# Four streams on one core: masked copy on ScalarE, division on GpSimd, a shorter root, ternary weights on VectorE, and a written-out order of work

## The reference, cut to what matters

```
x = x + tanh(g_xattn[l]) * attention_l(ctx, layernorm(x))
x = x + tanh(g_ffn[l])   * ffn_l(layernorm(x))
```

```
h = gelu(bitlinear(x, w1, b1)); y = bitlinear(h, w2, b2)
bitlinear: xn = x * rsqrt(mean(x*x) + 1e-6)
           xq = round(xn * 127 / max|xn|) ...;  wq = clip(round(w / mean|w|), -1, 1) * mean|w|
```

## Time and profile before

| | |
|---|---|
| time, median of 3 runs | 2720.06 us (2715.66 to 2722.37) |
| profiled execution, its own time | 2716.3 us |
| its span, first to last instruction | 2714.5 us |
| PE busy | 2508.9 us, 92% |
| DVE busy | 1688.8 us, 62% |
| ACT busy | 1041.0 us, 38% |
| POOL busy | 976.1 us, 36% |
| granted TensorE clock, mean | 0.975 |

### The profile page before, as it was taken

One profiled execution on the slowest core, in us unless ns is written; L12 is line 12 of the kernel. 1 busy time (PEld: TensorE's weight loads), 2 busy tenths in 40 slices (PEclk: granted clock), 3 DMA queues, 4 the chain that ended last, 5 costly groups with the idle time before them and its releaser, 6 DMA issues.

```text
span 2714.5 us, 53760 instructions
## 1 busy us (share of the span) xinstructions
PE 2508.9 (92%) x21317; PEld 1693.2 (62%) x21317; DVE 1688.8 (62%) x4598; ACT 1041.0 (38%) x1654; POOL 976.1 (36%) x2413
## 2 busy tenths in 40 slices
PE   6999788999999988899999998889999998889999
PEld 4566444677767644577776754457776765446776
DVE  6545888755533588955543478885554358887542
ACT  4544345432234445523224444542322444453221
POOL 2352522444332332243442243233444323224342
PEclk8999889999999999999999999999999999899999
DMA  3200100000000000000000000000000000000000
GB/s 125 81 11 1 52 32 14 1 9 9 9 9 12 12 2 14 1 1 9 9 9 9 11 12 1 12 1 9 9 9 9 11 1 12 1 1 1 5 5 8
DMA packets 16280, 37.38 MB, mean 14 GB/s; under 512 B 1408, under 2 KB 11424, under 8 KB 15008
## 3 DMA queue, kind: packets, MB, share of 16 engines
q1 hardware_dynamic: 16032, 33.94, 3.5%
HBM read 29.74 MB, written 4.19 MB: 13 GB/s over the span
## 4 chain that ended last, share of the span: by engine, by line
PE 69%; DVE 22%; ACT 4%; issue 3%; POOL 2%; DMA 0%; SPq 0%; DVEq 0%; ACTq 0%; POOLq 0%
PE P L1322 8%; PE P L1134 4%; PE P L1142 4%; PE P L1181 4%; PE P L1355 4%; PE P L1323 4%; PE P L1193 4%; PE P L1340 4%; PE P L1114 4%; PE P L1331 4%; PE P L1035 4%; DVE mx L1721 4%; PE P L1206 3%; PE P L1031 2%; PE P L1044 1%
## 5 line engine op out<-in xcount | busy, mean ns | idle before, releaser
L1721 DVE TENSOR_REDUCE mx<-P 128x8 f32<-128x1232 f32 x256 | 369.0, 1441 | 178.1 <-PE P L1040 85.9
L1322 PE MATMUL P<-xT,w 128*128 128x256 f32 x1024 | 264.8, 381 | 0.7 <-DVE R L1956 0.3
L1477 ACT ACTIVATE ET<-P 128x2048 f32<-128x2048 f32 x96 | 180.2, 1877 | 162.4 <-PE P L1117 115.3
L1772 DVE SCALAR_TENSOR_TENSOR x<-P,w_first,x 128x512 f32<-128x512 f32 x96 | 73.9, 769 | 252.8 <-PE P L1181 87.0
L1322 PEld LDWEIGHTS P<-xT,w 128*128 128x128 f32 x1024 | 192.0, 190 | 60.7 <-issue 34.9
L792 POOL TENSOR_TENSOR sm<-sm 128x2 f32<-128x2 f32 x384 | 76.0, 198 | 421.0 <-DVE sm L1717 401.0
L1949 DVE SCALAR_TENSOR_TENSOR gu<-gu,P 128x256 f32<-128x256 f32 x128 | 53.9, 421 | 256.7 <-ACT gu L1528 256.7
L1035 PE MATMUL P<-KB,R 32*128 32x308 f32 x1536 | 162.0, 492 | 34.5 <-ACT ET L1477 14.7
L1528 ACT ACTIVATE gu<-P 128x256 f32<-128x256 f32 x128 | 49.2, 384 | 355.9 <-PE P L1323 334.4
L1114 PE MATMUL P<-R,KB 32*128 32x256 f32 x2048 | 169.6, 417 | 14.9 <-DVE mx L1721 14.8
L1434 ACT ACTIVATE xn<-x,sm 128x256 f32<-128x256 f32 x256 | 139.1, 592 | 100.9 <-POOL sm L800 100.9
(11 more groups left out here) (307 smaller groups left out, 5580.8 us busy)
## 6 DMA issues: line engine op xcount, KB each, us to landing
kvw<-in_wkv SPq DMA_DIRECT2D x12, 672.0 KB, 3.9
x<-in_x SPq DMA_DIRECT2D x16, 256.0 KB, 2.8
out<-x SPq DMA_DIRECT2D x16, 256.0 KB, 2.1
w<-in_w SPq DMA_DIRECT2D x2, 1024.0 KB, 5.9
w<-in_wexp SPq DMA_DIRECT2D x1, 1028.0 KB, 7.6
w_w<-in_wcon SPq DMA_DIRECT2D x1, 1024.0 KB, 9.9
w_w<-in_m3t SPq DMA_DIRECT2D x1, 1024.0 KB, 8.3
w<-in_w1q SPq DMA_DIRECT2D x1, 1024.0 KB, 10.3
```

What stands on the lines that cost most here:

```text
L1322: e.matmul(o, wm[:, c, js], s.xT[:, c, :], start=n == c == 0, stop=False, skip_group_check=True)
L1477: e.activation(ET[:].rearrange("p g c -> p (g c)"), quad.rearrange("p g c -> p (g c)"), ACT.Exp, bias=mb1[:, b:b + 1] if l == 1 else 0.0). ...
L1721: e.tensor_reduce(s.mx[:, i, :, 2 * u:2 * u + 2], quad[:, :, 0:2 * NK].rearrange("p g (a k) -> p g a k", a=2), AX.X, ALU.max).then_inc(q_d, 1)
```

## The change

1. `no` in layers 1 to 3 is split. DVE's part ends with the first transpose. A new part of ACT copies the two halves of the bank, each under its mask column, into a new tile VS in the stream's scratch, which frees the bank; one VS serves both halves u, so the second copy waits for POOL's product of the first. A new stage `nz` has the reciprocals and the transpose back on DVE, and a product of 128x512 and the sum of the halves on POOL.
2. The root in `gelu2` works on -x/2 as `norm` does, and each of its steps is done for the two rows of a partition in instructions of one element, so that an instruction waits for the last but one and not for the one ahead of it.
3. `tern` is whole on DVE; SP and PE wait for `d_quant` in place of `g_tern`.
4. The order of each queue no longer comes from `BACK`. A string for each engine (`TURN`) names, item by item, the stream whose next item goes into that engine's queue. The strings came from a local search with new costs in `parts`. A stream may have 64 items open, not 24, stage `val` no longer follows `key` in the plan, and `fill` may also go into the first part of the kernel.

```diff
+            s.VS = part(512, [512])
...
+        TURN = {
+            "PE":
+                "0323232002323232322322010222200110330331030030310130202210012111112120323212102302123222323221032231"
...
-                while i in live and len(queue[i]) < 24:
+                while i in live and len(queue[i]) < 64:
...
-                i, p = min(can, key=lambda c: (start(c[1]) + BACK[c[1][2]].get(c[1][1], 0) + 130.0 * count[c[0]] + 34.0 * c[0],
-                                               count[c[0]] + 0.3 * c[0]))
+                i, p = min((c for c in can if TURN[c[1][2]][taken[c[1][2]]] == str(c[0])), key=lambda c: start(c[1]))
+                taken[p[2]] += 1
...
-                if p[2] == "PE" and at - free["PE"] > 900.0 and done.get("folded") and let["bank"]:
+                if p[2] == "PE" and at - free["PE"] > 900.0 and let["bank"]:
...
-            def tern(c):
-
-                raw, to = ((w1r, w1i), (w2r, w2i))[c]
-                e.wait_ge(d_quant, c + 1)
-                e.tensor_scalar(raw, raw, wsc[:, 4 + c:5 + c], MAGIC, ALU.mult, ALU.add).then_inc(g_tern, 1)
-                e.wait_ge(g_tern, 3 * c + 1)
-                e.tensor_scalar(raw, raw, -MAGIC, 1.0, ALU.add, ALU.min).then_inc(g_tern, 1)
-                e.wait_ge(g_tern, 3 * c + 2)
-                e.tensor_scalar(to[:].rearrange("p a b -> p (a b)"), raw, -1.0, None, ALU.max).then_inc(g_tern, 1)
...
+            def nz(s, b, l, u):
+                t = s.Z[u]
+                e.wait_ge(s.d_o, C.up(s.d_o))
+                e.wait_ge(s.a_q, 13 * b + 3 * l + 3 + u)
+                e.tensor_tensor(t, t, s.VS, ALU.mult).then_inc(s.g_z, 1)
+                e.wait_ge(s.g_z, C.up(s.g_z))
+                e.tensor_tensor(s.OT[:, u, :], t[:, 0:256], t[:, 256:512], ALU.add).then_inc(s.g_p, 1)
                 C.up(s.g_p)
...
-                    free[k] = [(s.d_o, X.up(s.d_o))]
+                    X.up(s.d_o)
+                    X.up(s.d_a)
+                    free[k] = [(s.a_q, X.up(s.a_q))]
...
+            def no(s, b, l, u, k):
+
+                e.wait_ge(s.d_a, C.up(s.d_a))
+                if u:
+
+                    e.wait_ge(s.g_z, 10 * b + 3 * l)
+                for a in range(2):
+                    t = e.activation(s.VS[:, 256 * a:256 * a + 256], P[:, k, 256 * a:256 * a + 256], ACT.Copy,
+                                     scale=tm[:, 2 + a:3 + a])
+                t.then_inc(s.a_q, 1)
...
+                e.tensor_scalar(raw, raw, wsc[:, 4 + c:5 + c], MAGIC, ALU.mult, ALU.add).then_inc(d_own, 1)
+                e.wait_ge(d_own, C.up(d_own))
+                e.tensor_scalar(raw, raw, -MAGIC, 1.0, ALU.add, ALU.min).then_inc(d_own, 1)
+                e.wait_ge(d_own, C.up(d_own))
+                e.tensor_scalar(to[:].rearrange("p a b -> p (a b)"), raw, -1.0, None, ALU.max).then_inc(d_quant, 1)
...
+                if l:
+                    e.transpose(t, bank).then_inc(s.d_a, 1)
+                    C.up(s.d_a)
+                    return
...
-                    for a in range(2):
-                        h = t[:, 256 * a:256 * a + 256]
-                        t_ = e.scalar_tensor_tensor(out=h, in0=bank[:, 256 * a:256 * a + 256], scalar=tm[:, 2 + a:3 + a],
-                                                    in1=h, op0=ALU.mult, op1=ALU.mult)
-                    t_.then_inc(s.d_o, 1)
...
+            def nz(s, b, l, u):
+                t = s.Z[u]
+                T, z = t.rearrange("p (a b c) -> p a b c", a=2, c=32), s.z[:].rearrange("p (a b) -> p a b", a=2)
+                e.wait_ge(s.d_a, C.at(s.d_a))
+                C.up(s.g_z)
+
+                for a in range(2):
+                    e.reciprocal(z[:, a, :], T[:, a, :, 16 - 16 * a]).then_inc(d_own, 1)
+                e.wait_ge(d_own, C.up(d_own, 2))
+                e.transpose(t, s.z[:].unsqueeze(2).broadcast_to([128, 16, 32])).then_inc(s.d_o, 1)
...
+                def own(t, of):
+
+                    t.then_inc(d_own, 1)
+                    e.wait_ge(d_own, C.up(d_own) - of)
+
...
+                own(e.tensor_scalar(hv, ss, 1.0 / 1024.0, 1e-6, ALU.mult, ALU.add), 0)
+                own(e.tensor_scalar(a.bitcast(i32), hv.bitcast(i32), 1, None, ALU.logical_shift_right), 0)
+                own(e.tensor_scalar(hv, hv, -0.5, None, ALU.mult), 1)
+                own(e.tensor_scalar(y.bitcast(i32), a.bitcast(i32), -1.0, 1597463007.0, ALU.mult, ALU.add), 0)
+                for n in range(3):
+                    for i in range(2):
+                        own(e.tensor_scalar(a[:, i:i + 1], y[:, i:i + 1], y[:, i:i + 1], hv[:, i:i + 1], ALU.mult, ALU.mult), 1)
+                    for i in range(2):
+                        own(e.tensor_scalar(y[:, i:i + 1], a[:, i:i + 1], 1.5, y[:, i:i + 1], ALU.add, ALU.mult), 1)
+
+                for i in range(2):
+                    own(e.tensor_scalar(am2[:, i:i + 1], am2[:, i:i + 1], y[:, i:i + 1], 1e-5, ALU.mult, ALU.max), 1 - i)
+                own(e.reciprocal(f, am2), 0)
+                own(e.tensor_scalar(sq, am2, wsc[:, 7:8], None, ALU.mult), 1)
+                for i in range(2):
+                    own(e.tensor_scalar(f[:, i:i + 1], f[:, i:i + 1], 127.0, y[:, i:i + 1], ALU.mult, ALU.mult), 1 - i)
```

More of the change, by code:

```diff
@@ L326, in late @@
                 return [("near", of[0], of[1] - 2)]
+            if engine == "POOL" and name == "no" and of[2] == 0:
+                return [("values", of[3])]
+            if name == "no" and engine == "ACT" and of[3]:
+                return [("divided",)]
+            if name == "nz" and engine == "POOL":
+                return [("copied", of[3])]
             if name == "hw" and of[1] == 6:
@@ L354, in early @@
                 return name, *of
+            if engine == "ACT" and name == "pv":
+                return "values", of[3]
+            if engine == "ACT" and name == "no":
+                return "copied", of[3]
+            if engine == "POOL" and name == "nz" and of[3] == 0:
+                return ("divided",)
             if engine == "DVE" and name in ("h1", "h2"):
@@ L531, in turns @@
                 yield "store", s, b
-        BACK = {"PE": {"back": 258, "down": 825, "exa": 222, "f3": 142, "gate1": -1154, "gate3": 710, "grow": -1683,
-                "h1": 298, "h2": -1734, "key": -1624, "lin": 1269, "mt": -537, "mw": -879, "near": 945, "out":
-                -1537, "pv": 383, "pz": 419, "q1": 260, "q2": -420, "qp": -3861, "sc": 286, "st": 693, "sts": 548,
-                "tsum": -183, "turn": -148, "up": 827, "upt": 383, "val": -555, "w1": -2247, "w2": -497},
-                "ACT": {"ex": 20, "gate1": -307, "gate3": 416, "gelu2": 1098, "h1": 335, "h2": 899, "key": -414,
-                "mt": 268, "mw": -3456, "near": 1412, "norm": 1319, "pv": -616, "q1": 2008, "q2": 944, "qp": 695,
-                "sts": 33, "tl": 802, "turn": 715, "up": -563, "val": 1578, "wide": 1273},
-                "DVE": {"down": 2589, "e3": -1428, "exa": 312, "f3": -1372, "gate1": 1049, "gate3": 95, "gb": -1063,
-                "gelu2": 3285, "grow": -1183, "h1": -3449, "h2": 365, "lin": 1331, "masks": -170, "mx": 917, "near":
-                1117, "no": 1568, "norm": 181, "out": 588, "q1": 1272, "q2": 1256, "split": 990, "tern": -1664,
-                "top1": 2363, "tsum": -740, "upt": -438, "val": 1642, "w1": 708, "w2": 1204, "wide": 1172},
-                "POOL": {"bias": 3534, "hw": -2455, "key": 2928, "mw": 1867, "no": 1720, "norm": 348},
-                "SP": {"kvw": -673, "late": -842, "store": -1615}}
@@ L851, in hw @@
                 C.up(s.g_p)
-            stages = {"key": key, "norm": norm, "bias": bias, "no": no, "mw": mw, "hw": hw, "tern": tern}
+            stages = {"key": key, "norm": norm, "bias": bias, "no": no, "nz": nz, "mw": mw, "hw": hw}
             for name, *of in ORDER["POOL"]:
```

169 lines of the change are left out of this document (98 added, 71 removed).

## The result

The changed kernel takes 2702.7 us (median of 5 runs, 2698.2 to 2707.8) against 2719.3 before (5 runs, 2715.6 to 2722.4): a ratio of 0.9943, 95% interval 0.9925 to 0.9961. It is faster by 16.6 us, a quarter of the 65 forecast, and lies 0.7 us above the forecast's range. Of the cases that were written down it is nearest to the rival in which POOL's products take back what the split gives (2690).

What follows compares the result with a forecast made beforehand. It took DVE to set the pace in the dips and PE elsewhere. 33 (DVE relief) + 7 (`tern`) + 25 (order) = 65 us off 2716.3 gave 2651, forecast as a 2655 us median, range 2600 to 2702.

Steps and rivals of the forecast that it cites:

- the rival in which POOL's products take back what the split gives: POOL's products hold DVE at SBUF, 60 x 0.8 us, cancelling the 48 us: 2690 us, chance 0.19.
- The relief: `no` split: two products of 0.80 us a pair leave DVE, 60 pairs in the dips, 48 us.
- the dips: Four stretches, 870 us together, streams in attention 2 and 3 and feed-forward 1 and 2; DVE 88% busy, PE has gaps.
- the factor of 0.7: Share of DVE's relief in the dips counted for the end: 47 us become 33, bounds 0.3 and 1.
- One product of POOL can thus cost DVE between 0 and 1.27 us. I take 0.2.: POOL's new product in `no` stalls small DVE SBUF instructions: 60 x 0.2 = 12 us, bounds 0 and 76.
- The path from bank to OT grows from 3.5 us to about 3.9.: Split `no`: POOL's product takes 1.27 us where DVE's took 0.80; a few us of PE waiting, not priced separately.
- The third rival: Hand-offs exposed at the end of 48 attentions in layers 1 to 3, 2 us each: 2751 us, slower, chance 0.09.
- The root: `gelu2` on DVE: overlapping small steps take 3.0 us, 0.7 less, x 16 = 11 us, all in the dips.
- `tern`: Ternary weights on DVE, 4.4 us for three passes, POOL no longer holding DVE: 7 us, bounds 2 and 15.
- The lists: Written-out queue order and early `fill`: a tenth of 245 us of PE gaps and `fill`, 25 us.
- In the dips DVE sets the pace: DVE is nearly full there while 199 us are free of useful PE work; outside them PE sets the pace.
- The bounds: Limits on the end's gain from DVE work removed in the dips: 5 to 69 us around 33.

Runs made afterwards that it cites:

- experiment 8: Changed kernel with POOL's product cut to 2 columns, plus POOL zeros or scratch products: behind the halves' sum 2673.9 or 2683.5 us, ahead of it 2685.0 or 2690.8.

## Why the prediction was wrong

The step that failed is the split of `no` with its order, above all in the two prices that it put on the detour over ACT and POOL: a path of 3.9 us, which is 7.3, and 8 us at the end for POOL's product, whose removal moves the end by 26. The forecast booked 48 us off DVE less 12 for POOL's hold, times 0.7, 25 us gained, and 25 more for the order. Measured, the split with its order loses 18 us against the same kernel without both (2702.7 and 2680.9, ratios 0.9943 and 0.9877). The runs don't divide this loss between the two. Point by point:

- *The relief.* "60 pairs x 0.80 = 48 us": with the products cut to 2 columns the end moves by 17 us for 30 of DVE in the dips, but PE's wait behind the same path shrank by 10, so the factor of 0.7 is neither confirmed nor refuted.
- *"One product of POOL can thus cost DVE between 0 and 1.27 us. I take 0.2."* DVE's busy time falls by 20.3 us when the product goes, 0.21 for each of 96: the price was right. What it does to the end was not. The forecast took it as 60 x 0.2 x 0.7 = 8 us. Narrowing the product moves the end by 26, of which products that nobody waits for reproduce 9, and products in its place 15. Some 15 of the profiled 27.5 us are PE's own matmuls at a higher granted clock, a term that the sum did not have.
- *"The path from bank to OT grows from 3.5 us to about 3.9."* It grew to 7.3. The sum added durations of instructions and no queues: DVE, ACT, DVE and POOL in turn, each with other streams' work in front. A microsecond more of zeros on each pair's path costs 11 us at the end (experiment 8). "I leave it in the factor below" was the mistake.
- *The third rival* has this mechanism and said that it decides from 1.35 us for each attention. In the old order the kernel is 95 us slower, with PE 61 us in front of `out`; in the new order that wait is 2.7 us.
- *The root.* Forecast 11 us off the stage and 8 at the end. Measured, 14 off the stage alone and 21 in the changed kernel, and 27 and 19 at the end. The overlap of the steps was the smaller part: without a stall the stage went from 3.80 to 3.48 us, not by the 0.7 forecast. The larger part was not in the sum: the 3.70 us of the old root left out one stalled instruction as an exception, and stalls were the rule (5.05 us on average, 12 of 16 turns stalled). The new root is stalled for less of its time. At the end, 10 of the 24.6 us between the profiled executions are shorter gaps and 14 are PE's own matmuls at a higher granted clock; what raised the clock is not shown. One factor of 0.7 for everything on DVE did not hold.
- *`tern`.* Forecast 7, measured 10 (7 to 14). Right, with its reasons.
- *The lists.* Forecast 25 us and a few from the clock. The early filling gives 6. The rest of the order can't be priced apart from the stages; what it shows is that it hides the split's path (61.3 us of PE's wait down to 2.7), and beyond that no gain appeared in the dips.
- *"In the dips DVE sets the pace"* did not hold as it stands. DVE's narrow products and its root gained time, but each also shortened a path that PE waits for, so they don't tell load from path. In the changed kernel DVE's time fell by 38 us with PE's gaps unchanged, while the stage's own path grew.
- *The bounds.* "With the bounds above 5 to 69": the 5 does not follow. With POOL's price at its own bound of 76 the split alone stands at 48 - 76 = -28 us, so the sum allowed for a loss that its range left out.

So the sum would have read: root 27, `tern` 10, filling 6, less 10 of overlap, less 18 for the split with its order, 15 us in all. The 65 forecast had 50 us on the split and the order.

## What to carry to other kernels

Work that is moved off a busy engine is a chain with one more hand-off for each engine it visits. Price the queue in front of each, from the mean of all instances of the stage and not from the sum of its instructions. Read a stage's time as the mean over all its instances, stalls included, for the instance that looks undisturbed is the one that misleads. And take each part of a change apart before keeping it: here three small parts are worth 33 us, and the large one takes 18 back. Where the granted clock can move, compare PE's own matmul time beside its gaps before a cause is named.

## What the runs showed of the hardware

VectorE `tensor_scalar` instructions on one element, with scalars from columns, were not held by POOL: all 96 of L1907 took 262 to 275 ns, and of the new root's one-element instructions in that kernel 69 overlapped in time with a POOL instruction of two SBUF operands. On two elements a `tensor_tensor` of the old root lasted up to 1194 ns where its median is 161, and a `tensor_scalar` with a scalar from a column (L1914) had a median of 1012 ns where its shortest took 228. 100 us of zeros filled in by POOL behind the sum left VectorE's busy time at 1609.0 us (1611.3 without); ahead of the sum it was 1615.9. ACT's 192 copies out of PSUM take 258 ns with 2 columns and 470 with 256, and the time did not change between them. And TensorE's filling is worth 21 and 26 us in the two kernels through the granted clock (0.960 to 0.975, and 0.964 to 0.983), though it computes nothing.
